# Setup, embedding and layers of a decoder block in one program, with the input norm as centred weights and a scale on the product

## What is computed

```python
x = x + attn(layernorm(x))          # the part that is changed
x = x + xattn(layernorm(x), ctx)    # ctx: 8 x 256 x 1024; needs, per position, the top-k mask over 256 channels
x = x + moe(layernorm(x))           # 2 of 8 experts, 1024 x 1024 each

def attn(x):                        # DIM 128, 4 layers
    h = x @ Win.T + bin             # embedding, 1024 -> 128
    for each layer:
        y = silu(layernorm(h) * w + b)
        y = causal_convolution(y)   # per channel, with powers of one complex number
        h = h + y * scl
        h = h + W2 @ silu(W1 @ layernorm(h) + b1) + b2
    return layernorm(h) @ Wout.T + bout
```

## Time and profile before

| | us |
|---|---|
| median of 3 runs | 1268.26 |
| lowest and highest | 1267.88 and 1272.83 |
| profiled execution, device time | 1264.29 |
| span in its trace | 1262.4 |
| setup, from the start to the first instruction of the embedding | 0 to 19.85 |
| embedding | 19.85 to 92.69 |
| layers | 92.96 to 465.06 |
| the rest (second and third part) | to 1262.4 |

### The profile page before, as it was taken

One profiled execution on the slowest core, in us unless ns is written; L12 is line 12 of the kernel. 1 busy time (PEld: TensorE's weight loads), 2 busy tenths in 40 slices (PEclk: granted clock), 3 DMA queues, 4 the chain that ended last, 5 costly groups with the idle time before them and its releaser, 6 DMA issues. The chain is left out here.

```text
span 1262.4 us, 14138 instructions
## 1 busy us (share of the span) xinstructions
PE 1035.2 (82%) x3383; PEld 574.5 (46%) x3384; DVE 578.5 (46%) x1626; ACT 401.9 (32%) x1268; POOL 516.8 (41%) x691
## 2 busy tenths in 40 slices
PE   3875898888988537852798579999999999999995
PEld 2534554554544213431798534444444444444442
DVE  4764456778897776773784521111121112111110
ACT  1322568577786407674562000000000000000000
POOL 3752466556664302211660063344334433433441
PEclk8986898789898669875775579999999999999998
DMA  3503110100000417710457233637363736454332
GB/s 119 175 29 129 43 42 1 51 34 34 1 1 1 115 47 175 165 33 0 183 223 295 116 80 87 200 70 220 76 199 76 219 71 199 88 148 130 71 87 42
DMA packets 41003, 128.60 MB, mean 102 GB/s; under 512 B 6715, under 2 KB 9846, under 8 KB 40950
## 3 DMA queue, kind: packets, MB, share of 16 engines
q0 software_dynamic: 15120, 48.25, 18.1%
q1 hardware_dynamic: 25830, 79.77, 17.6%
HBM read 82.91 MB, written 36.70 MB: 95 GB/s over the span
## 5 line engine op out<-in xcount | busy, mean ns | idle before, releaser
L1882 PE MATMUL bank<-T,X 128*128 x1184 | 511.0, 594 | 13.9 <-DVE X L1920 10.8
L1882 PEld LDWEIGHTS bank<-T,X 128*128 128x128 f32 x1184 | 225.7, 191 | 298.6 <-issue 298.6
L1934 DVE TENSOR_SCALAR X<-bank,col_p 128x512 f32<-128x512 f32 x37 | 27.8, 751 | 410.0 <-PE bank L1882 410.0
L1900 ACT ACTIVATE X<-bank,col_p 128x512 f32<-128x512 f32 x37 | 25.4, 687 | 523.6 <-PE bank L1882 523.6
L1835 POOL DMA_INDIRECT X<-x_nrm,col_s x156 | 149.4, 958 | 98.7 <-DVE col_s L1925 51.4
L1844 POOL DMA_INDIRECT out_dram<-X,col_d x37 | 59.8, 1615 | 269.3 <-DVE X L1934 218.8
L904 ACT ACTIVATE M<-X,T 128x256 bf16<-128x256 f32 x224 | 110.4, 497 | 10.1 <-POOLq L650 10.0
L342 POOL TENSOR_TENSOR rs<-ve,neg_half 128x1 f32<-128x1 f32 x48 | 34.6, 721 | 145.7 <-DVE ve L338 145.4
L645 POOL TENSOR_TENSOR T<-T 128x8 f32<-128x8 f32 x216 | 87.4, 405 | 16.3
L654 POOL TENSOR_TENSOR rs<-ve,neg_half 128x4 f32<-128x4 f32 x36 | 39.6, 1101 | 109.5 <-DVE ve L1005 109.5
L796 PE MATMUL bank<-nat,T 128*128 128x512 f32 x128 | 80.1, 772 | 4.6 <-issue 2.7
(11 more groups left out here) (282 smaller groups left out, 1504.0 us busy)
## 6 DMA issues: line engine op xcount, KB each, us to landing
T<-in_L_ffn_expert_w_dram SPq DMA_DIRECT2D x8, 4096.0 KB, 17.6
out_dram<-X SPq DMA_DIRECT2D x17, 512.0 KB, 3.3
nat<-in_x_dram SPq DMA_DIRECT2D x16, 512.0 KB, 4.5
X<-in_x_dram SPq DMA_DIRECT2D x16, 512.0 KB, 4.3
X<-late POOLq DMA_DIRECT2D x16, 512.0 KB, 5.4
x_nrm<-H SPq DMA_DIRECT2D x16, 512.0 KB, 2.7
T<-in_ctx_dram SPq DMA_DIRECT2D x12, 512.0 KB, 3.7
X<-x_nrm,col_s POOLq DMA_INDIRECT x156, 3.6
```

The source lines that it names most:

```text
L1882: mm = nc.tensor.matmul(bank[2 * u + n][:, :], xgt[u][:, k, :], Tf[:, ds(odd * (KD * D) + (k * D + n * BANK), BANK)], start=(k == 0), stop ...
```

## The change

The three blocks become one. There is no meeting of the engines after the setup and none after the embedding.

- **The input norm.** The tiles of `x` are no longer normed before the product. `Win` is centred over its 1024 inputs (statistics and one subtraction on VectorE, lines 1061 to 1066 of the new code), so the mean of a row drops out of the product. The statistics of `x` are still taken, four tiles at a time (`x_stats`), one power of four columns per chunk (`power_x`), and TensorE spreads the scale over a bank (`spread`, 4 products of 128 columns) as it does for the layers' norms. ScalarE copies that bank out, VectorE multiplies the embedding's product by it and adds the bias in a second instruction (`embedded`).
- **The product** is taken tile by tile, 8 products of 128 columns each, in place of 8 of 512 columns per chunk. Two tiles of turned `x` are held, not all.
- **Slots.** `FIRST` is -4. Chunk `q` is embedded in slot `q - 4`, so the loops run over `range(-4, 21)`. The layers' visits keep their slots. The batches of `ctx` keep their places after `FIRST` and so come two slots earlier beside the visits.
- **Loads.** Eight tiles of `x` can be under way at once (`RING`, in the space of `M`), in place of four. `Wout` and the first batches of `ctx` come between them, the gate's weights later.
- **Other moves.** GpSimd builds the tables in slots -4 to -2. VectorE makes the two bands at the ends of slots 0 and 1 (`taps`). In slot 0 ScalarE does the high counts and the third counts of batch 0 in full.

```diff
-        FIRST = -2
+        FIRST = -4
...
+                def embedded(t):
+                    q, u = divmod(t, TPC)
+                    if u == 0 and q > 0:
+                        pe.wait_ge(e_h, q)
+                    pe.wait_ge(emb_tpev, 2 * t + 2)
+                    for k in range(KD):
+                        mm = nc.tensor.matmul(bank[OB][:, u * P:(u + 1) * P], win_t[:, k, :], x_t[t % 2][:, k, :], start=(k == 0), stop=(k == KD - 1))
+                    mm.then_inc(emb_mm, 1)
...
+                def embedded(q):
+                    dve.wait_ge(emb_mm, q * TPC + TPC)
+                    dve.wait_ge(e_bcs, q + 1)
+                    v_.tensor_tensor(chunk(H, q), bank[OB][:, :], chunk(sq, q), ALU.mult).then_inc(e_h, 1)
+                    hold(dve, e_h, q + 1)
+                    v_.tensor_scalar(chunk(H, q), chunk(H, q), block_par[:, 0:1], None, ALU.add).then_inc(emb_ev, 1)
...
+                for s in range(FIRST, SLOTS_END):
+                    if 0 <= s + 4 < CH:
+                        power_x(s + 4)
+                    if s < -1:
+                        for m in range(*((0, 4), (4, 7), (7, 8))[s + 4]):
+                            doubled(1 << m)
...
+                    if s < 0:
+                        if 0 <= s + 2:
+                            silu(s + 2)
+                        copies(b0, 2 * h0)
+                        act.wait_ge(emb_ev, s + 5)
+                        square(s + 4, sq1)
+                        copies(b0, 2 * h0 + 1)
...
+                    if s == 0:
+                        act.wait_ge(h_mid, s + 1)
+                        square(s, sq2)
+                        count_high(0, 0, KD)
+                        silu(s + 2)
+                        copies(b0, 2 * h0)
+                        copies(b0, 2 * h0 + 1)
+                        count_third(0, 0, KD)
+                        continue
...
+                    if s in (0, 1):
+                        taps(s)
```

More of the change, by code:

```diff
@@ L115, in decoder_kernel @@
         w1u = in_t(FF)
-        rows = in_t(P)
+        rows_raw = in_t(P)
         ph = in_t(4 * NL).rearrange("p (k l) -> p k l", k=4)
@@ new lines, in _ @@
+                sp.dma_start(nat[:, 0, :], w_in[:, :]).then_inc(ld_win, 16)
+                for t in range(5):
+                    row(t)
+                sp.dma_start(wo_raw.rearrange("p (t d) -> p t d", t=KD), w_out.rearrange("(t p) d -> p t d", p=P)).then_inc(ld_wout, 16)
+                for t in range(5, RING):
+                    row(t)
+                sp.dma_start(bout_b, b_out.rearrange("(a d) -> a d", a=1).to_broadcast([P, D])).then_inc(ld_bout, 16)
+                context(0)
+                for t in range(RING, RING + 4):
+                    row(t)
@@ L715, in _ @@
                 ins.then_inc(sel_pool, 1)
-                for s in range(-2, SLOTS_END):
-                    if s + 2 < FINAL:
+                pool.wait_ge(set_dve, 20)
+                for s in range(FIRST, SLOTS_END):
[4 more added lines that the diff above has]
+                            doubled(1 << m)
+                    if 0 <= s + 2 < FINAL:
                         power(s + 2, ve1, rt1)
-                    if starts(s, 4) is not None:
+                    if s > 0 and starts(s, 4) is not None:
                         third_threshold(starts(s, 4))
@@ new lines, in embedded, with embed @@
+                def embedded(t):
[6 more added lines that the diff above has]
+                    mm.then_inc(emb_mm, 1)
+                def embed(q):
+                    for u in range(TPC):
+                        t = q * TPC + u
+                        if t + 1 < NT:
+                            x_turned(t + 1)
+                        embedded(t)
+                    pe.wait_ge(e_rt, q + 1)
+                    if q > 0:
+                        pe.wait_ge(e_bcs, q)
+                    spread(q, ZB, e_bc)
@@ new lines, in taps @@
+                def taps(c):
+                    if c == 0:
+                        dve.wait_ge(ld_misc, NMISC * 16)
+                    banded(v_.tensor_scalar(band[:, c, :], ewide[:, 0:3 * P], convw[:, c * TAPS:c * TAPS + 1], None, ALU.mult))
+                    for j in range(1, TAPS):
+                        w_ = convw[:, c * TAPS + j:c * TAPS + j + 1]
+                        banded(v_.scalar_tensor_tensor(band[:, c, :], ewide[:, j:j + 3 * P], w_, band[:, c, :], ALU.mult, ALU.add))
+                dve.wait_ge(const_ready, 16)
@@ L1085, in _ @@
+                link(v_.tensor_copy(quarter[:, :], io_part))
+                link(v_.tensor_scalar(later_t[:, :], step_t[:, :, :].rearrange("p e t -> p (e t)"), 0.0, None, ALU.is_gt))
+                for s in range(FIRST, SLOTS_END):
                     b1, h1 = batch_at(s, 1)
```

554 lines of the change are left out of this document (277 added, 277 removed).

## The result

| | before | after |
|---|---|---|
| median of the first runs (5 each) | 1269.28 | 1235.3 |
| lowest and highest | 1267.88 and 1273.92 | 1220.63 and 1240.1 |
| ratio, with its 95% interval | | 0.969 [0.965, 0.973] |
| six more runs of the same kernel: median | | 1238.67 |
| their ratio to 11 more runs of before | | 0.9725 [0.9692, 0.9759] |

The ratios are taken over the runs and are not the quotients of the medians, which are 0.973 and 0.976; the first leaves out the run of 1240.1, which is 1.6% above the fastest. By medians and ratios the change makes the kernel faster by 31 to 39 us, some 3%. I had forecast 25. By the ratio of the six further runs it is 1233, inside the range, so the low figure hangs in part on one fast run.

What follows compares the result with a forecast made beforehand. No engine full in setup and embedding, TensorE and VectorE near full in the slots, VectorE's search alone at the end; front +15.3, slots and tail sum to 25.0 gained, 1239.3 profiled, 1243 us as median; range 1231 to 1259.

Steps and rivals of the forecast that it cites:

- The front: Setup and embedding up to visit 0's middle: gains 15.3 us, bounds 9 to 18, with middle 0 at 110.6.
- the three turnovers: Between embedding chunks: 5.9 us each for copies, scale and hand-overs, with 4 more for layer 0's preparation before chunk 3.
- Rival 2: Embedding: idle turnovers cool TensorE, 5.5 tiles at the lower clock cost 16 us; gain 12, 1256 us; chance 0.15.
- Rival 3: Embedding never gets the full clock, 43 us more; kernel takes 1286 us; chance 0.07.
- rival 4: Embedding's 128-column passes cost 260 ns, not 131, even at full clock; 33 us more, 1276 us; chance 0.03.
- Slot 0: First layer slot: ScalarE's counts and wait for GpSimd's threshold delay the hidden layer; 21.1 us, -5.3.
- Slot 1: VectorE makes a band (`taps`) at the slot's end, on the path to the middle; -4.3 us.
- Slots 2 to 4: Selection moved two slots earlier gives these slots the load of slots 4 to 6; -5.5 us, bounds 0 and -8.
- rival 1: Layer slots swallow the moved work: slot 0 and slots 2 to 4 cost nothing; gain 35.8, 1232 us; chance 0.14.
- Slots 5 to 14: Alike as before, except slots 12 and 13 lose their turns of `ctx`; +2 us, bounds 0 and 4.
- The tail and the last norm: After the last visit: two of four search groups gone, +17.4 us; last square behind 8 counts, not 16, +3.4.
- what I had named as late next: After the last norm: still VectorE's search; loads of `x` and GpSimd's bias adds finish within it.

Runs made afterwards that it cites:

- experiment 9: Changed kernel with each tile's eight embedding products of 128 columns issued twice; one run took 1257.98 us.
- experiment 6: Changed kernel with ScalarE copying the next chunk's first tile before the spread, and VectorE scaling chunk 0 before chunk 1's statistics; median 1230.84, 0.9685.
- experiment 5: Changed kernel with both bands made on VectorE in slot -1, none in slots 0 and 1; median 1237.83, 0.9735.
- experiment 3: Changed kernel with the selection back at its old place beside the visits, so the front alone; median 1250.37, 0.9809.
- the second trace of after: Profile of another run of the unchanged changed kernel; 1239.46 us, against the first trace's 1220.63.
- second pair of traces: Second traces of the unedited kernels: before, a run of 1269.61 us; after, a run of 1239.46 us.
- experiment 1: The changed kernel run again without edit; six runs of 1229.94 to 1239.46, median 1238.67.
- products with zeros: Extra TensorE products adding nothing, four at each of two places per slot from 2 on; changed kernel 1233.8, 0.9716; kernel before 1262.25, 0.9927.
- the last version: Changed kernel with third counts moved, bands in slot -1, shorter turnover, and products with zeros in three stretches per slot; median 1220.65, 0.9588.
- the three edits alone: Changed kernel with third counts behind the first hidden layer, both bands in slot -1 and the shorter turnover; median 1226.58, 0.9674.

## Why the prediction was too slow

**The front: the term that was mis-sized.** I put a tile at 1.09 + 2.1 = 3.2 us, the sum of two listed durations. Its pitch, from start to start, is 2.66, of which the products are 1.79 (experiment 9), so 16 tiles are 8.6 us too dear. This is the step that failed: listed durations were added, though each reaches over the start of the next group. The trace of before had it: there too the row behind a spread starts 0.89 after it, though the spread is listed with 1.05. Smaller parts went the same way: chunk 0 was done 1.0 earlier than its tiles explain, and the spreads (0.89 and not some 1.1) and the last tile, which has no turn behind it, took 1.5 less. Others went against it: the three turnovers took 3.9 more (the first stood behind VectorE's statistics of the next chunk, whose place in the order I had not taken into the sum, experiment 6), and 4.0 in place of 3 went to two tiles at the lower clock. So chunk 3's scale was spread at 92.41, 6.2 before my 98.6, and the last step, from there to middle 0, took 10.3 where I had 12. Together these are the 7.9 us by which the front was off.

**Rival 2** had its mechanism right and its size wrong: turnovers did cool TensorE, for one tile each behind the first and the third (the second, 4.9 long, did not), 4.0 us in all and not 16. Rival 3 fell: of 16 tiles 14 ran at the full clock. So did rival 4: 16 passes of 128 columns go in 1.79 us, 112 ns each, a quarter of the 446 ns of a pass of 512 columns. The ratio of 2.5 between four short matmuls and one long one, my estimate from the two figures of the Trainium skill in "TensorE: Matmul & The Clock Gate", "Back-to-back issue gap", is 1.0 here.

**The slots.** Slot 0: the right place, -8 to -10 for -5.3; the threshold's steps took 5.7 and not 4.58, beside the band that I had called covered. Slot 1: -4.3 for the band alone was too dear. Without it the slot was 0.6 shorter at a lower clock and 1.2 at the same one (experiment 5), since the late hidden layer sets it too. Slots 2 to 4: priced from whole slots of before (41.1 against 37.3) whose clocks differed, 0.83 in both of the longer pair against 0.83 and 0.90 in the other. At like clock it is -1.8, nearer to rival 1's nothing than to my 5.5; for slot 0 rival 1 fell. Slots 5 to 14: the forecast of +2 can't be told from the clock's scatter; only slot 13 shows it, 18.5 in experiment 3 and 16.8 in the second trace of after. Over slots 0 to 14 I had -13.1, and the two pairs of traces show -2.0 and -16.6.

**The tail and the last norm** were right to 0.2 us, and so was what I had named as late next: everything behind the block starts 44.4 (29.9) earlier and takes the same. GpSimd's tables ended at 61.5, hidden:

```profile
52.91 8.56 POOL L417 TENSOR_TENSOR T<-T 128x512 f32<-128x512 f32 x11
```

**The sum.** The second pair of traces gives 30.3 us between two runs near their medians (by device time 30.2): my 25.0, 9.5 more from the front, 3.5 less from slots 0 to 14, 0.7 less from the rest. That the first ratio went below my range has a second cause: my range took in the terms' bounds, but not that two runs of one kernel differ by up to 19 us. What I left out is the clock's fall inside the slots (15.4 of 18.9 us in the pair of experiment 1), though the earlier trace rows and the clock of whole slots of before show it.

**What stays open.** What makes the clock fall in more slots in one run of a kernel than in another; where the kernel before gains by the products with zeros; the stretch behind the layers, which differed by up to 12 us between these traces (789.5 to 801.8) and which no experiment touched; and how much of the last version's gain is the filled stretches at all, since its interval overlaps that of the three edits alone: its block ended 5.5 earlier (419.81 and 425.29), and behind it it took 4.0 more.

## What to carry to other kernels

Take the price of a pipelined group from the distance between starts, not from the listed duration: the difference was 0.54 us in 3.2, 16 times over. Before pricing a stretch from another one that holds more work, put the granted clock of both beside it; and take a second trace before explaining a few microseconds. Where an engine's clock falls behind sparse stretches, a wait can cost more than its own length, and filling it is worth a try; but look in the trace whether the time was gained where the filling stands.

## What the runs showed of the hardware

- Eight products with zeros in a slot made the kernel before faster, 0.9927 [0.9899, 0.9954], though its one trace doesn't show the gain in the slots. Fourteen held the granted clock at 1.00 in all of slots 5 to 14, which took 176.0 us in place of 188.7 with the three edits alone. Slots 6, 7, 10 and 11 of the changed kernel took 2.0 to 2.6 us longer at a mean clock of 0.83 than at 0.90 to 0.91, slot 5 only 0.2 longer at 0.82 than at 1.00.
- Sixteen passes of 128 columns took 1.79 us from start to start at the full clock, 112 ns each, though they are listed with 1.95.
- GpSimd's nine steps of 128 x 8 took 5.7 us beside VectorE's two-input band and 3.9 without.
